# Layers 3 and 4 of a four-layer graph network: turning and scoring all nodes first, thirteen projections beside the factors, node sums from turned nodes, bias in the last sweep

## What is computed

```python
# L2: two heads of 128 features
xt = einsum('nf,hfo->hno', x, W)
e1, e2 = einsum('hno,ho->hn', xt, a1), einsum('hno,ho->hn', xt, a2)
scores = leaky_relu(e1[:, :, None] + e2[:, None, :], 0.2)
scores = where(adj + eye > 0, scores, -9e15)
out = elu(einsum('hij,hjo->hio', softmax(scores, -1), xt))
# L3: four heads of 64 features, over the other axis of adj, with a bias
h = (x @ W).reshape(n, 4, 64)
s_src, s_dst = einsum('nhc,hc->nh', h, a_src), einsum('nhc,hc->nh', h, a_dst)
e = leaky_relu(s_src[:, None, :] + s_dst[None, :, :], 0.2)
e = where((adj > 0.5)[:, :, None], e, -1e9)
out = einsum('ijh,ihc->jhc', softmax(e, axis=0), h).reshape(n, 256) + bias
```

## Time and profile before

| | us |
|---|---|
| three timed runs | 2113.03 to 2115.75, median 2114.61 |
| the profiled execution's own time | 2117.71 |
| its span in the profile | 2116.0 |
| PE busy | 2046.6 (97%) |
| DVE busy | 1526.1 (72%) |
| ACT busy | 970.4 (46%) |
| POOL busy | 89.7 (4%) |

### The profile page before, as it was taken

The page is one execution under the profiler, slowest core; times in us unless marked ns, Lnnn a source line. Parts: engine busy times, 40 slices in busy tenths (PEclk is TensorE's granted clock), DMA queues, the critical chain, the costliest instruction groups (busy, mean ns, idle before and its releaser), DMA issues.

```text
span 2116.0 us, 28365 instructions
## 1 busy us (share of the span) xinstructions
PE 2046.6 (97%) x10838; PEld 1156.1 (55%) x10847; DVE 1526.1 (72%) x2511; ACT 970.4 (46%) x1517; POOL 89.7 (4%) x113
## 2 busy tenths in 40 slices
PE   7999998799999998999999999999999999999997
PEld 4555665344444454555555544455899985333343
DVE  4665556798988877544578894344589987999988
ACT  3222224698988878755222220000411326654555
POOL 0000000000000000000000010000000102000000
PEclk9999999899999999999999999999999999999999
DMA  7665654355564554654000015444100004333331
GB/s 237 210 210 190 199 182 178 143 205 191 179 227 168 198 184 144 224 172 135 20 0 1 0 35 135 131 127 110 54 1 2 1 1 182 115 87 110 84 88 56
DMA packets 124647, 260.14 MB, mean 123 GB/s; under 512 B 14643, under 2 KB 54121, under 8 KB 121929
## 3 DMA queue, kind: packets, MB, share of 16 engines
q1 hardware_dynamic: 106185, 228.95, 34.0%
q10 hardware_dynamic: 18324, 29.34, 3.7%
HBM read 217.66 MB, written 40.59 MB: 122 GB/s over the span
## 4 chain that ended last, share of the span: by engine, by line
PE 72%; DVE 17%; ACT 6%; issue 2%; DMA 1%; POOL 0%; SPq 0%; DVEq 0%; ACTq 0%
PE banks L1083 21%; PE banks L1136 10%; PE banks L1170 9%; PE banks L986 9%; PE banks L1215 8%; PE banks L1234 4%; PE banks L975 3%; DVE arena L2300 3%; DVE arena L1832 2%; ACT arena L1361 2%; PE banks L889 2%; PE banks L1027 2%; DVE arena L1913 1%; DVE arena L2016 1%; DVE arena L2017 1%
## 5 line engine op out<-in xcount | busy, mean ns | idle before, releaser
L1083 PE MATMUL banks<-arena 128*128 128x512 f32 (+2 forms) x1512 | 583.2, 544 | 17.3 <-DVE arena L1913 17.2
L1083 PEld LDWEIGHTS banks<-arena 128*128 128x128 f32 x1512 | 282.8, 190 | 308.3 <-issue 229.1
L1913 DVE TENSOR_TENSOR arena<-arena 128x1536 f32<-128x1536 f32 (+4 forms) x132 | 201.9, 1529 | 150.2 <-ACT arena L1397 134.3
L2300 DVE SCALAR_TENSOR_TENSOR arena<-arena 128x1024 f32<-128x1024 f32 (+3 forms) x264 | 288.3, 1165 | 10.2 <-PE banks L1234 9.2
L1170 PE MATMUL banks<-arena 128*128 128x129 f32 (+1 forms) x1936 | 221.2, 276 | 3.5 <-DVE arena L2199 3.1
L986 PE MATMUL banks<-arena 128*128 128x512 f32 (+4 forms) x528 | 223.8, 545 | 0.2 <-ACT arena L1302 0.2
L1170 PEld LDWEIGHTS banks<-arena 128*128 128x128 f32 (+1 forms) x1936 | 217.8, 192 | 7.1 <-DVE arena L2199 3.8
L1215 PE MATMUL banks<-arena 128*32 128x512 f32 (+1 forms) x2112 | 215.5, 545 | 3.0 <-DVE arena L2300 3.0
L1136 PE MATMUL banks<-arena 128*128 128x512 f32 (+4 forms) x528 | 206.0, 544 | 1.2 <-DVE arena L2008 1.2
L1832 DVE CUSTOM_DVE_ANT_0 arena<-arena 128x2708 f32<-128x2708 bf16 (+1 forms) x66 | 196.2, 2973 | 2.2 <-DMA arena<-e_rows 1.9
L1397 ACT ACTIVATE arena<-arena 128x1536 f32<-128x1536 f32 (+4 forms) x132 | 170.6, 1292 | 57.3 <-DVE arena L1895 57.0
(11 more groups left out here) (245 smaller groups left out, 2197.1 us busy)
## 6 DMA issues: line engine op xcount, KB each, us to landing
arena<-hw_rows SPq DMA_DIRECT2D x126, 384.0 KB, 3.1
arena<-adj_T SPq DMA_DIRECT2D x126, 256.0 KB, 3.3
arena<-in_adj SPq DMA_DIRECT2D x17, 1354.0 KB
arena<-in_adj SPq DMA_DIRECT2D x42, 512.0 KB
adj_T<-arena ACTq DMA_DIRECT2D x63, 256.0 KB, 2.2
arena<-adj_T SPq DMA_DIRECT2D x84, 192.0 KB, 2.9
arena<-in_adj SPq DMA_DIRECT2D x15, 1024.0 KB
arena<-in_adj SPq DMA_DIRECT2D x15, 768.0 KB
```

The lines of the kernel that those rows point to most:

```text
L1083: ins = PE.matmul(bank(2 * (c % 2) + f)[:, 0:wid(c)], hs[0:R, m % 3, h * D + f * P:h * D + (f + 1) * P], weights_of(n)[0:R, h, 0:wid(c)], ...
L1913: V.tensor_tensor(e, e, a, ALU.mult).then_inc(s["p_ok"], 1)
L2300: V.scalar_tensor_tensor(PM3[0:k, n % 3, h, 0:w], r3_bc[0:k, h, c * WW:c * WW + w], smalls[0:k, 4, h * T + t:h * T + t + 1], mask3[0:k, n ...
```

## The change

Both projection stages are split at tile 9 of the order (`SOONER`). Tiles 0 to 8 are turned and projected as before. Tiles 9 to 21 are first only turned, and multiplied with the score columns alone (`score`); their scores gather in one PSUM bank and DVE copies them together (`later_scores`). Only then come the thirteen products of 256 columns, behind the engines' arrival at the barrier and beside DVE's factors. They rotate over three banks. `pe_rows` stands behind the fifth of them. DVE copies them out after its factors; in layer 4 the last two copies stand between the second and the third head of the first unit of the sweep. For this the turned tiles are all kept: in `tmp` in layer 3, in the place of `g3` in layer 4.

The node sum is taken another way. The 22 matmuls with ones go. ACT sums the turned tiles over the nodes (`nodes_summed`: two activations with `accum_out` over 22 x 128 columns, then two that widen the sums to 128 columns), and PE multiplies that by the weights (`node_sums`), at unit 2 of the sweep. In layer 3 ACT does this ahead of its scaling; in layer 4 ahead of `degree_weights`, and copies the result at unit 4. The last tile of `g3` is cleared on ACT.

The bias of layer 4 is added two tiles at a time in units 2 to 12 of chunk 0 (`biased`), no more in the stage. In layer 4 the finishing of layer 3's last tiles stands at earlier places of the tile loop, and both normalisings come after tile 8's product.

```diff
-        def pe_project(pe, i, wcat, cols, between=None):
...
+        def product_bank(q):
+
+            return bank(2 * (q % 2) if q < SOONER else (3, 2, 0)[(T - 1 - q) % 3])
...
-            def product(q):
+            def product(q, cols):
                 t = order[q]
                 pe.wait_ge(xt_ok, q + 1)
-                if q >= 2:
+                if q >= SOONER:
+                    pe.wait_ge(proj_ok, max(SOONER, q - 2))
+                elif q >= 2:
                     pe.wait_ge(proj_ok, q - 1)
                 for kk in range(KD):
-                    ins = PE.matmul(bank(2 * (q % 2))[0:kp(t), 0:cols], xT[:, q % 2, kk, 0:kp(t)], wcat[:, kk, 0:cols],
+                    ins = PE.matmul(product_bank(q)[0:kp(t), 0:cols], turned[i][:, q, kk, 0:kp(t)], wcat[:, kk, 0:cols],
                                     start=kk == 0, stop=kk == KD - 1)
                 ins.then_inc(proj_ps, 1)
 
-            def node_sum(q):
+            def score(q):
                 t = order[q]
-                pe.wait_ge(proj_ok, q + 1)
-                rhs = proj2[0:kp(t), t, :, 0:C2] if i == 1 else proj3[0:kp(t), t, 0:D]
-                PE.matmul(bank(4)[:, 0:D], ones[0:kp(t), :], rhs, start=q == 0, stop=q == T - 1).then_inc(sum_ps, 1)
+                pe.wait_ge(xt_ok, q + 1)
+                for kk in range(KD):
+                    ins = PE.matmul(score_bank(i, heads)[0:kp(t), t, :], turned[i][:, q, kk, 0:kp(t)], wcat[:, kk, D:D + 2 * heads],
+                                    start=kk == 0, stop=kk == KD - 1)
+                return ins
...
-            for t in range(T):
-                if t + 1 < T:
-                    turn(t + 1)
-                product(t)
-            if i:
-                arrive(pe, "pe")
-                if i == 2:
-                    pe.wait_ge(l2_read, CH)
-                for q in range(ROWS_FROM):
-                    node_sum(q)
-                pe.wait_ge(fg_ok, i)
-                k, heads = (None, ("r2", H2), ("r3", H3))[i]
-                pe_rows(k, smalls[:, 6, 0:heads * T], heads)
-                for q in range(ROWS_FROM, T):
-                    node_sum(q)
-                all_here(pe, "pe")
+            for q in range(SOONER):
+                turn(q + 1)
+                product(q, D + 2 * heads)
+            for q in range(SOONER, T):
+                if q + 1 < T:
+                    turn(q + 1)
+                ins = score(q)
+            ins.then_inc(xt_ps, 1)
+            arrive(pe, "pe")
+            for q in range(SOONER, T):
+                product(q, D)
+                if q == SOONER + 4:
+                    pe.wait_ge(fg_ok, i)
+                    pe_rows((None, "r2", "r3")[i], smalls[:, 6, 0:heads * T], heads)
+            all_here(pe, "pe")
+
+        def node_sums(pe, i, wcat):
+
+            pe.wait_ge(projs[i][1], T + 3)
+            for kk in range(KD):
+                ins = PE.matmul(bank(6)[:, 0:D], sums_wide[:, kk, :], wcat[:, kk, 0:D], start=kk == 0, stop=kk == KD - 1)
+            ins.then_inc(sum_ps, 1)
 
...
+                if n == 0:
+                    pe.wait_ge(projs[1][3], T)
+                if n == 2:
+                    node_sums(pe, 1, wcat2)
...
+                    else:
+                        pe.wait_ge(projs[2][3], T if h else T - 2)
...
-                        pe.wait_ge(l3_g, 1)
-                        pe.wait_ge(sum_ok, 2)
+                        pe.wait_ge(l3_g, 2)
...
+                if n == 2:
+                    node_sums(pe, 2, wcat3)
...
+        def nodes_summed(act, i):
+            xt_ok = projs[i][1]
+            act.wait_ge(xt_ok, T)
+            for kk in range(KD):
+                S.activation(unread[i][:, kk * T * P:(kk + 1) * T * P].rearrange("p (t n) -> p t n", t=T), turned[i][:, :, kk, :], ACT.Copy,
+                             accum_out=sums_x[:, kk:kk + 1]).then_inc(xt_ok, 1)
+            act.wait_ge(xt_ok, T + 2)
+            for kk in range(KD):
+                ins = S.activation(sums_wide[:, kk, :], ones, ACT.Copy, scale=sums_x[:, kk:kk + 1])
+            ins.then_inc(xt_ok, 1)
...
@@ -1506,8 +1549,9 @@
             factors(0, H2)
             act_rows(act, "r2", H2)
             all_here(act, "act")
+            nodes_summed(act, 1)
             for t in range(T):
-                act.wait_ge(sum_ps, t + 1)
+                act.wait_ge(projs[1][3], t + 1)
...
-            act_project(act, 2, {1: whole_scaled, 2: last_negative, 4: mixed_negative, 5: last_positive, 6: last_exponentials,
-                                 8: lambda: roots_2(CH - 2), 13: lambda: roots_2(CH - 1)})
+            act_project(act, 2, {1: whole_scaled, 2: last_negative, 3: mixed_negative, 4: last_positive, 5: last_exponentials,
+                                 7: lambda: roots_2(CH - 2), 10: lambda: roots_2(CH - 1)})
...
             def degree_weights():
+                act.wait_ge(projs[2][2], SOONER + 2)
+                S.activation(g3[:, T - 1].rearrange("p h d -> p (h d)"), ones, ACT.Copy, scale=0.0).then_inc(l3_g, 1)
+                act.wait_ge(l3_g, 1)
...
             def scaled_tile(t):
                 nr = kp(t)
+                act.wait_ge(projs[2][3], ORDER.index(t) + 1)
...
             above(0)
             masked(0)
+            scaled_tile(0)
+            nodes_summed(act, 2)
             degree_weights()
-            scaled_tile(0)
-            sums_copied(act, 2)
             for n in range(1, UNITS3):
...
+                if n == 4:
+                    sums_copied(act, 2)
...
+        def later_scores(dve, i, heads, dst):
+
+            dve.wait_ge(projs[i][0], T + 1)
+            for nr, ts in LATER:
+                ins = V.tensor_copy(dst[0:nr, ts, :], score_bank(i, heads)[0:nr, ts, :])
+            return ins
...
+            V.memset(turned[1][:, T - 1], 0.0)
+            features2 = (proj2[:, :, :, 0:C2], 0, D)
+            for q in range(SOONER):
+                if q == 4:
+                    last_normed()
+                projected(dve, 1, q, (features2, (score2, D, D + 2 * H2)))
             arrive(dve, "dve")
+            dve.wait_ge(projs[1][3], SOONER)
+            link(later_scores(dve, 1, H2, score2))
             factors(0, H2, score2[:, :, 0:H2], score2[:, :, H2:])
+            for q in range(SOONER, T):
+                projected(dve, 1, q, (features2,))
             all_here(dve, "dve")
...
-            dve_project(dve, 2, ((proj3, 0, 0, D + 2 * H3),), {
-                2: mixed, 7: lambda: last_added(T - 3), 8: lambda: last_added(T - 2), 9: lambda: last_added(T - 1),
-                10: lambda: batch_normed(CH - 2, slice(0, 2)), 11: lambda: batch_normed(CH - 2, slice(2, 4)),
-                15: lambda: batch_normed(CH - 1, slice(0, 1)), 16: lambda: batch_normed(CH - 1, slice(1, 3))})
+            soon = {1: mixed, 5: lambda: last_added(T - 3), 6: lambda: last_added(T - 2), 7: lambda: last_added(T - 1)}
+            for q in range(SOONER):
+                if q in soon:
+                    soon[q]()
+                projected(dve, 2, q, ((proj3, 0, D + 2 * H3),))
+            batch_normed(CH - 2)
+            batch_normed(CH - 1)
             arrive(dve, "dve")
+            dve.wait_ge(projs[2][3], SOONER)
+            link(later_scores(dve, 2, H3, proj3[:, :, D:]))
             factors(1, H3, proj3[:, :, D + H3:], proj3[:, :, D:D + H3])
-            dve.wait_ge(projs[2][0], T)
-            for nr, ts in FULL:
-                x = xnat[0:nr, ts, :]
-                V.tensor_tensor(x, x, b3_bc[0:nr].unsqueeze(1).to_broadcast([nr, ts.stop - ts.start, D]), ALU.add)
+            for q in range(SOONER, T - 2):
+                projected(dve, 2, q, ((proj3[:, :, 0:D], 0, D),))
...
+            def biased(v):
+                for nr, ts in pair_parts(v):
+                    x = xnat[0:nr, ts, :]
+                    ins = V.tensor_tensor(x, x, b3_bc[0:nr].unsqueeze(1).to_broadcast([nr, ts.stop - ts.start, D]), ALU.add)
+                link(ins)
...
+                    if n == 0 and h == 2:
+                        for q in range(T - 2, T):
+                            projected(dve, 2, q, ((proj3[:, :, 0:D], 0, D),))
                     V.scalar_tensor_tensor(PM3[0:k, n % 3, h, 0:w], r3_bc[0:k, h, c * WW:c * WW + w],
                                            smalls[0:k, 4, h * T + t:h * T + t + 1], mask3[0:k, n % 3, 0:w],
                                            ALU.max, ALU.mult).then_inc(l3_p, 1)
+                if c == 0 and 2 <= t < 2 + PAIRS:
+                    biased(t - 2)
```

More of the change, by code:

```diff
@@ L864, in _, with score_bank, pe_project @@
             pool.sem_inc(parts_ok, 1)
-        def pe_project(pe, i, wcat, cols, between=None):
+        turned = [None, tmp.rearrange("p t (k n) -> p t k n", k=KD),
+                  arena[:, g3_at:g3_at + T * D].rearrange("p (t k n) -> p t k n", t=T, k=KD)]
+        unread = [None, tmp2.rearrange("p t d -> p (t d)"), PM3[:, 1:3].rearrange("p n h w -> p (n h w)")]
```

(10 more changed lines are left out.)

45 lines of the change are left out of this document (21 added, 24 removed).

## The result

Eight timed runs of the changed kernel have a median of 2122.5 us (2121.12 to 2127.64), eight of the kernel before on the same chips 2116.59 us; the ratio is 1.0029 (95% interval 1.0018 to 1.0040). So the change makes the kernel slower by 0.3%, about 6 us. The profiled execution took 2125.4 us, its span is 2123.7 us: 7.7 us more than before on both counts.

What follows compares the result with a forecast made beforehand. PE, busy 97% of the span, was taken as the bound. Layer 3 at -1.3 and layer 4 at +2.0 gave +0.7, 2115.3 us; clock falls of 8.2 made it 2123.5 us, range 2110.5 to 2127.0.

Steps and rivals of the forecast that it cites:

- Scoring, 0.68 us a tile: Tiles 9 to 21, turned and scored with no product between: 0.68 us a tile, ends 0.52 and 0.85.
- Layer 3, steps 1 to 3: Layer 3's stage: last score 5.5 us earlier, then +3.3 from the later transpose and the products and copies behind it.
- second step: Layer 3, last score to transpose: PE stands at product 12 for a bank; 5.7 us instead of 3.7, +2.0.
- the signs: Expected in the trace if right, among others PE idle 1.3 to 2 us ahead of product 12.
- third step: Layer 3, transpose to sweep: DVE's start waits for the last products and copies, not a DMA; +1.3.
- Node sums, +0.9 on PE: Layer 3: ACT's sums cost nothing, with 2 us of cover; on PE four records at unit 2 add 0.9 us.
- Layer 4, step 3: Layer 4, ahead of unit 1: ACT's second mask ends at 20.5 us, DVE stands from 18.7; +4.5 less 6.3, 1.8 earlier.
- The bias, unit 13 at +2.0: Layer 4, units 2 to 12: eleven additions, 7.9 us, make DVE exceed PE; less lead of 4.1 and 1.8, +2.0.
- The sign that I gave, 0.3 to 0.5 us a unit: Layer 4, units 2 to 13: DVE without idle and PE waiting 0.3 to 0.5 us a unit for it.
- The rival in which DVE's lead covers the additions: Layer 4, chunk 0: PE stays the bound and the clock holds; layers -3.4 and -1.3, 2109.9 us; chance 0.15.
- The clock, 4.1 us a layer: Both scoring stages: granted clock falls to half in the middle; 4.1 us a layer, 8.2 in all; chance 0.50.
- The rival "the clock holds": Both scoring stages keep the full clock: 2115.3 us, 2111.1 to 2119.7; chance 0.32.

Runs made afterwards that it cites:

- fed: Changed kernel plus one matmul of 512 bf16 columns behind each score but the last, in both layers; 2120.8 us, ratio 1.0016 to the kernel before.
- mixed: Changed kernel with the nine products ahead of the last score spread over all 22 turns; 2117.5 us, ratio 1.0005 to the kernel before.
- filled: Changed kernel with mixed order, 12 products, earlier rows' transpose and second mask, bias partly in scoring, eight 512-column matmuls before each sweep; 2109.5 us, 0.9964 of the kernel before.
- no bias: Changed kernel without the eleven additions of the bias in units 2 to 12 of layer 4's sweep; 2118.4 us, ratio 1.0004 to the kernel before.
- bias in scoring: Changed kernel with eight bias additions on DVE during layer 4's scoring, three in units 6, 10 and 14; 2118.4 us, ratio 0.9999 to the kernel before.
- 15 products: Changed kernel with 15 products ahead of the last score instead of 9; 2122.6 us, ratio 1.0030 to the kernel before.

## Why the prediction was right

The forecast was 2123.5 us for a median before of 2114.6, +8.9; the runs gave 2122.5 for 2116.6, +5.9. That the absolute number is only 1.0 off is luck: the kernel before came out 2.0 slower in the eight runs than in the three that I had. In the profiled executions it was +7.7: the sum of the table rose by 8.3, and layer 3's first product began 0.6 earlier, since the fall at 1475.8 did not come this time. The other 1.8 us between +7.7 and +5.9 lie between executions: the changed kernel's profiled one is 2.9 us over its median, that of the kernel before 1.1, and I carried the difference over as if it were the same. Point by point:

- **Scoring, 0.68 us a tile.** 0.67 at full clock. It is the loop's limit: in the fed run a turn and a score take PE 0.21 and 0.37 us (1489.68, 1489.89, 1490.26), 0.58 together. An estimate from the Trainium skill (TensorE: Matmul & The Clock Gate, LDWEIGHTS) made a score 0.43 us; the row has 0.37 from the score at 1493.61 to the turn behind it.
- **Layer 3, steps 1 to 3, -2.2 us until the sweep with the clock held.** The mixed kernel has -2.6 (33.8 for 36.4). The second step's mechanism is there: the wait ahead of product 12 is 0.76 us (1.24 in layer 4, both in the fed run), not the 1.3 to 2 that I wrote among the signs, and the transpose comes 5.6 us after the last score in the fed run (1504.65), against 5.7. In the changed kernel itself no such wait is seen, because the products ahead of it ran at half clock. In the third step DVE's first sweep instruction follows the last copy, with no wait on a DMA in between.
- **Node sums, +0.9 on PE, no cost by ACT in layer 3.** 0.9 in layer 3, 1.1 in layer 4, and two activations of 2.55 us with 0.19 each for the sum, as named (ACT's timeline, the first of the two in layer 4):

```profile
1776.90 2.55 ACT L1315 ACTIVATE arena<-arena 128x2816 f32<-128x2816 f32 x1
```

- **Layer 4, step 3.** ACT's second mask does end last ahead of unit 1, by DVE's timeline:

```profile
1787.96 9.66 DVE L2375 SCALAR_TENSOR_TENSOR arena<-arena 128x1024 f32<-128x1024 f32 x8 [1.43 <-ACT arena L1670]
```

- **The bias, unit 13 at +2.0.** The fed run, with 1.6 us of filler taken off, has unit 13 at 112.8 us after the stage's start (37.9 + 76.5 - 1.6); before it was 110.8 (40.8 + 70.0): +2.0. The mechanism was right: DVE without idle, and PE short of 5.1 us in eleven units. The sign that I gave, 0.3 to 0.5 us a unit, holds for units 8 to 12 (0.35 each, 5.51 less 5.16); units 2 to 4 lose nothing and units 5 to 7 lose 3.3 us together, as GpSimd's work falls there. The rival in which DVE's lead covers the additions is out: with the two slowed ones they cost 8.6 us of DVE (11 x 0.72 = 7.9 forecast), and the lead paid 3.5.
- **The clock, 4.1 us a layer.** It fell in the middle of both stages. Until the sweep the price was 3.3 to 3.4 us in layer 3 (fed, mixed) and 3.0 to 4.8 in layer 4. But that is not the net price, and here lies the step that was mis-sized: layer 3's term. A kernel that keeps its clock in layer 3's scoring lost it at the start of the sweep in every profiled execution but the filled one, which gives 1.6 us to the other side. Stage and sweep of layer 3 together are 262.0 us in the changed kernel, 260.2 in the mixed one and 260.3 in the fed one without its filler: 1.7 to 1.8 us, not 4.1. In the earlier trace rows the fall at 1783, behind a wait of 2.6 us, stood there for layer 4; I did not ask whether a scoring at full clock would bring one to layer 3's sweep. In layer 4 neither the fed nor the mixed kernel had such a fall, and unit 13 begins 4.2 and 2.4 us sooner after the stage's start than in the changed kernel. So the fall cost 4.2 to 5.9 us net by the table, and 5.0 by the timed medians of mixed and changed, not 8.2.

Added up by layers, the table has +1.7 us in layer 3, where -1.3 + 4.1 = +2.8 was forecast, +6.2 in layer 4 until unit 13, where 2.0 + 4.1 = +6.1 was, and +0.4 in the rest. That layer 4 fits to a tenth is partly luck: this execution had the clock low for 13.6 us there, three other kernels with the same scoring for 10.2, and two of these (no bias, bias in scoring) have a stage 2.3 to 2.4 us shorter.

The rival "the clock holds" gave 2115.3, 0.03% over the median before. The mixed kernel, in which it held through scoring, came to 1.0005. So the change would have gained nothing even then: what it takes from the stages, the bias and the node sums give back.

The Trainium skill's rule (same page, "Why this matters for your kernels") that there be no long idle gap between bursts would have made the rival in which the clock holds the forecast. The trace disagrees at the falls at 1495.5 and 1758.3, where PE's rows have no wait at all in the 4.6 and 3.9 us ahead. That idle time can bring a fall the runs bear out: the one behind PE's 2.2 us wait goes when the wait is filled. But a wait is not enough: in the changed kernel PE waits 2.2 us ahead of layer 3's sweep and 2.5 ahead of layer 4's, and the clock stays at 1.00 behind both.

## What to carry to other kernels

Work that is moved ahead to start a serial chain earlier should keep wide matmuls among the narrow ones; putting all narrow ones in one piece cost more than the chain gained, and the same instructions in mixed order did not. Before an addition is moved off a stage into a sweep, compare the other engine's unit with the new one and count its lead; a wait of the same engine (here DVE's 7.3 us for the scores) is the better place. And a stage that keeps its clock may lose part of the gain to a fall behind the next wait; look for it in the trace of the kernel that keeps it.

## What the runs showed of the hardware

- The granted clock fell to 0.50 while PE was recorded busy for every bit of the 4.6 and 3.9 us ahead, with turns and matmuls of 4 or 8 columns; with one matmul of 512 bf16 columns added to each 0.8 us it stayed at 1.00, and so it did with one product in each two or three tiles (fed, mixed).
- A fall came also when thin work ended (15 products: at 1503.2, behind 4.1 us of scoring), so that it hit full products; how long a fall lasted was 3.4, 6.8, 10.2 or 13.6 us, and differed between executions of the same code (in layer 4's scoring 13.6 in the changed kernel, 10.2 in the kernel without the bias).
- With eight matmuls on zeros in the wait of 2.2 us the clock stayed at 1.00 behind it and nothing was lost that a row shows (one profiled execution).
- While GpSimd worked, DVE's four heads took 5.82 and 6.26 us instead of 4.87, and the addition of 128x512 took 0.88 and 1.15 us instead of 0.68.
